# Two adaLN blocks on one core: clearing the probabilities of later keys on GpSimd, with all engines' orders written anew

## The reference

```
x = x + ga * attention0(norm(x))         # one head, no mask, softmax over 256 keys
x = x + gb * ffn0(norm(x))               # 128 -> 352 -> 128, inputs and weights rounded to blocks of fp4
x = x + ga * attention1(norm(x))         # 16 heads of 8, causal
x = x + gb * experts(norm(x))            # 4 experts of 704 in use, the best 2 weighted by a softmax
```

## Time and profile before

| | |
|---|---|
| median of 3 runs | 1906.71 us (1906.49 to 1907.74) |
| the profiled execution's own time | 1907.06 us |
| its span (first to last instruction) | 1905.3 us |
| full turns | 12, between 318.96 and 1635.28 us |
| GpSimd instructions | 78 |

### The profile page before, as it was taken

The page is one execution under the profiler, slowest core; times in us unless marked ns, Lnnn a source line. Parts: engine busy times, 40 slices in busy tenths (PEclk is TensorE's granted clock), DMA queues, the critical chain, the costliest instruction groups (busy, mean ns, idle before and its releaser), DMA issues.

```text
span 1905.3 us, 37018 instructions
## 1 busy us (share of the span) xinstructions
PE 1699.7 (89%) x12297; PEld 1317.1 (69%) x12297; DVE 1678.0 (88%) x3791; ACT 716.5 (38%) x1447; POOL 68.9 (4%) x78
## 2 busy tenths in 40 slices
PE   2347799999999999999999999999999999999998
PEld 1234567776776767677686767777676777768787
DVE  5578799989899998989989998999989899997775
ACT  0122435262533426253432526243352525334332
POOL 0000000000000000000000000000000000000000
PEclk7686899999999999999999999999999999999999
DMA  4020302003030301203030110303021030303000
GB/s 142 25 76 28 109 5 89 28 20 98 5 107 10 104 14 27 86 15 97 10 105 13 50 63 18 99 5 106 12 63 51 18 99 6 100 10 91 12 13 8
DMA packets 130106, 97.25 MB, mean 51 GB/s; under 512 B 28000, under 2 KB 124512, under 8 KB 125824
## 3 DMA queue, kind: packets, MB, share of 16 engines
q1 hardware_dynamic: 121536, 91.74, 16.4%
q10 hardware_dynamic: 8448, 4.20, 0.7%
HBM read 56.48 MB, written 29.98 MB: 45 GB/s over the span
## 4 chain that ended last, share of the span: by engine, by line
PE 47%; DVE 37%; issue 9%; ACT 4%; SPq 1%; DVEq 1%; DMA 1%; POOL 0%; ACTq 0%; POOLq 0%
DVE mneg L1099 9%; PE y_ps L1476 9%; PE bank L1469 5%; PE bank L1471 5%; PE bank L1470 5%; DVE h L1196 4%; PE bank L1220 4%; DVE tt L1188 3%; PE bank L1436 3%; ACT arena L770 2%; DVE xh L967 2%; PE bank L1343 2%; DVE arena L1107 2%; PE bank L1373 2%; PE bank L1420 2%
## 5 line engine op out<-in xcount | busy, mean ns | idle before, releaser
L813 ACT ACTIVATE tt<-bank 128x512 f32<-128x512 f32 x352 | 212.4, 603 | 665.8 <-PE bank L1471 523.9
L1476 PEld LDWEIGHTS y_ps<-wd,h 128*128 128x128 f32 (+1 forms) x3072 | 379.1, 192 | 70.7 <-issue 19.1
L1476 PE MATMUL y_ps<-wd,h 128*128 128x128 f32 (+1 forms) x3072 | 415.4, 282 | 14.1 <-DVE h L1196 14.1
L1196 DVE TENSOR_TENSOR h<-tt,bank 128x512 f32<-128x512 f32 x352 | 236.0, 682 | 23.6 <-PE bank L1471 7.1
L1188 DVE SCALAR_TENSOR_TENSOR tt<-tt,bank 128x512 f32<-128x512 f32 x352 | 237.2, 682 | 21.4 <-ACT tt L813 14.7
L1099 DVE TENSOR_REDUCE mneg<-bank 128x2 f32<-128x512 f32 (+1 forms) x384 | 236.0, 680 | 3.9 <-issue 2.4
L770 ACT ACTIVATE arena<-bank 128x512 f32<-128x512 f32 x384 | 196.5, 612 | 34.8 <-PE bank L1417 20.7
L1469 PE MATMUL bank<-h_hi,wg_hi 128*128 128x512 f32 x352 | 164.2, 466 | 10.3 <-DVE h_lo L1163 3.8
L1469 PE MATMUL bank<-h_hi,wu_hi 128*128 128x512 f32 x352 | 163.1, 463 | 8.4 <-DVE mneg L1099 8.3
L1107 DVE TENSOR_TENSOR arena<-arena,keep_k 128x1024 f32<-128x1024 f32 (+1 forms) x96 | 149.0, 1577 | 20.4 <-ACT arena L770 18.8
L1471 PE MATMUL bank<-h_lo,wg_hi 128*128 128x512 f32 x352 | 140.5, 399 | 0.0
(11 more groups left out here) (183 smaller groups left out, 2647.0 us busy)
## 6 DMA issues: line engine op xcount, KB each, us to landing
q_stack<-q_rows SPq DMA_DIRECT2D x16, 1024.0 KB, 4.8
k_stack<-k_rows SPq DMA_DIRECT2D x16, 1024.0 KB, 8.0
q_rows<-qk_halves SPq DMA_DIRECT2D x48, 256.0 KB, 2.8
k_rows<-qk_halves SPq DMA_DIRECT2D x48, 256.0 KB, 2.9
rows<-mod_rows SPq DMA_DIRECT2D x48, 128.0 KB, 3.0
rows<-mod_rows SPq DMA_DIRECT2D x16, 384.0 KB, 3.5
x_in<-in_L_attn_X SPq DMA_DIRECT2D x16, 256.0 KB, 2.8
vals<-arena SPq DMA_DIRECT2D x128, 32.0 KB, 5.2
```

Source lines behind the costliest of these rows:

```text
L813: send(a(tt[:, ch % 2, :], ps.bank(f"eg{ch}")[:], ACT.Tanh, scale=0.5), tanh_ready)
L1196: frees(v.tensor_tensor(h32[:, ch % 3], tt[:, ch % 2, :], ps.bank(f"eu{ch}")[:], ALU.mult), f"eu{ch}")
L1476: ins = mm(y_ps[:, P * t:P * (t + 1)], h32[rows_, ch % 3, P * t:P * (t + 1)], wd[rows_, ch, :], start=first and t == 0, stop=last_ and t = ...
```

## The change

`cover` moves from VectorE to GpSimd. The table `keep_k` now holds 1 where the key is allowed and 0 elsewhere. A cover is now an addition of two 4-column constants into a tile `idle` that nobody reads, a minimum with 2.0 on the blocks, a wait until that is complete, and the product with the table.

```diff
-            v.tensor_scalar(keep_k[:], code_rowf, code_col[:], HUGE, ALU.is_ge, ALU.mult)
+            v.tensor_scalar(keep_k[:], code_rowf, code_col[:], 1.0, ALU.is_ge, ALU.mult)
...
-            def cover(it, u):
-
-                dve.wait_ge(*ps.is_freed(it, f"T{TURNED[u]}{GROUPS - 1}"))
-                n = S if TURNED[u] in EARLY else P
-                x = probs[:, GROUPS * (u % 3):GROUPS * (u % 3 + 1), :].rearrange("p g (h k) -> p (g h) k", k=n)[:, :, 0:P]
-                send(v.tensor_tensor(x, x, keep_k[:].unsqueeze(1).to_broadcast([P, GROUPS * 512 // n, P]), ALU.min), covered)
...
+            def cover(it, u):
+
+                pool.wait_ge(*ps.is_freed(it, f"T{TURNED[u]}{GROUPS - 1}"))
+                n = S if TURNED[u] in EARLY else P
+                x = probs[:, GROUPS * (u % 3):GROUPS * (u % 3 + 1), :].rearrange("p g (h k) -> p (g h) k", k=n)[:, :, 0:P]
+                g.tensor_tensor(idle[:], mhalf[:], mhalf[:], ALU.add)
+                send(g.tensor_scalar(x, x, 2.0, None, ALU.min), bounded)
+                pool.wait_ge(bounded.sem, bounded.at(it, u + 1))
+                send(g.tensor_tensor(x, x, keep_k[:].unsqueeze(1).to_broadcast([P, GROUPS * 512 // n, P]), ALU.mult), covered)
```

All five orders and `USES` are written anew. The turn is cut at another place: it begins at rows 2 of lead 1, and what stood before that in the old turn stands at the end of the turn before, with a lead one higher. The orders of SyncE and GpSimd:

```diff
-    do(1, "stack_v"), do(0, "load4"), do(1, "stack_max"), do(1, "load3"), do(1, "turn_att"), do(3, "load2"), do(4, "load1")
-    do(2, "store_q"), do(2, "store_k"), do(2, "stack")
+    do(1, "load3"), do(3, "load2"), do(0, "load4"), do(1, "turn_att"), do(2, "store_q"), do(4, "load1"), do(2, "store_k")
+    do(2, "stack"), do(2, "stack_v"), do(2, "stack_max")
...
-    do(2, "stats3"), do(1, "stats4"), do(3, "stats2"), do(4, "stats1")
+    do(1, "cover", 0), do(1, "cover", 1), do(1, "cover", 2), do(1, "cover", 3), do(1, "cover", 4), do(1, "cover", 5)
+    do(2, "stats3"), do(3, "stats2"), do(1, "stats4"), do(4, "stats1")
```

The new order of VectorE, its first third and its last lines:

```diff
+    do(3, "value0"), do(0, "swish", 10), do(0, "times", 10), do(0, "swish", 11), do(3, "scores0", 0), do(0, "mix", 1)
+    do(0, "times", 11), do(3, "scores0", 1), do(0, "swish", 12), do(2, "down0"), do(0, "swish", 13), do(0, "times", 12)
+    do(0, "times", 13), do(0, "swish", 14), do(1, "turn_out", 0), do(0, "times", 14), do(2, "stats3"), do(2, "norm3")
+    do(1, "turn_out", 1), do(1, "turn_out", 2), do(1, "turn_out", 3), do(0, "swish", 15), do(3, "out0"), do(3, "stats2")
...
+    do(1, "swish", 6), do(1, "swish", 7), do(1, "times", 6), do(3, "gate0", 3), do(1, "times", 7), do(3, "up0", 2)
+    do(1, "swish", 8), do(3, "up0", 3), do(4, "norm1"), do(1, "mix", 0), do(3, "quantise_h", 0, 2), do(1, "times", 8)
+    do(3, "quantise_h", 1, 0), do(3, "quantise_h", 1, 1), do(1, "swish", 9), do(1, "times", 9), do(3, "quantise_h", 1, 2)
```

The new order of TensorE, its first and its last lines:

```diff
+    do(1, "rows", 2), do(3, "scores0", 0), do(0, "down", 8), do(0, "gate", 10), do(0, "up", 10), do(0, "gate", 11)
+    do(2, "turn_h", 0), do(2, "turn_h", 1), do(1, "rows", 3), do(1, "weigh", 0), do(2, "turn_h", 2), do(0, "down", 9)
+    do(0, "down", 10), do(1, "rows", 4), do(1, "weigh", 1), do(0, "up", 11), do(2, "turn_h", 3), do(3, "scores0", 1)
+    do(1, "rows", 5), do(2, "down0"), do(0, "gate", 12), do(0, "gate", 13), do(0, "down", 11), do(3, "probs0", 0)
+    do(1, "turn_out", 0), do(0, "up", 12), do(0, "up", 13), do(0, "gate", 14), do(0, "up", 14), do(0, "gate", 15)
+    do(1, "weigh", 2), do(3, "probs0", 1), do(1, "turn_out", 1), do(1, "weigh", 3), do(1, "turn_out", 2), do(2, "turn3")
...
+    do(3, "gate0", 3), do(1, "gate", 7), do(1, "up", 6), do(1, "up", 7), do(1, "gate", 8), do(3, "up0", 2), do(1, "down", 5)
+    do(3, "up0", 3), do(1, "up", 8), do(1, "gate", 9), do(2, "rows", 0), do(1, "down", 6), do(1, "down", 7), do(4, "turn1")
+    do(2, "rows", 1), do(4, "key0"), do(4, "query0"), do(4, "value0"), do(1, "up", 9)
```

More of the change, by code:

```diff
@@ L44 @@
 NEG = -1.0e30
-HUGE = 3.0e38
 SCALE0 = float(P) ** -0.5
@@ L68 @@
 LOOPS = PAIRS - 1 - FIRST - LAST
-USES = [(1, "SB30", "D", 6), (1, "SB31", "D", 5), (1, "SB32", "D", 2), (1, "SB33", "D", 4), (2, "G3", "D", 6),
[23 rows of a table removed]
+USES = [(1, "TE10", "A", 0), (1, "TE11", "A", 1), (1, "TE12", "A", 5), (1, "TE13", "A", 6), (3, "S0", "A", 3),
[23 rows of a table added]
 def sp_order(do):
-    do(1, "stack_v"), do(0, "load4"), do(1, "stack_max"), do(1, "load3"), do(1, "turn_att"), do(3, "load2"), do(4, "load1")
-    do(2, "store_q"), do(2, "store_k"), do(2, "stack")
+    do(1, "load3"), do(3, "load2"), do(0, "load4"), do(1, "turn_att"), do(2, "store_q"), do(4, "load1"), do(2, "store_k")
+    do(2, "stack"), do(2, "stack_v"), do(2, "stack_max")
@@ L103, in pool_order @@
 def pool_order(do):
-    do(2, "stats3"), do(1, "stats4"), do(3, "stats2"), do(4, "stats1")
+    do(1, "cover", 0), do(1, "cover", 1), do(1, "cover", 2), do(1, "cover", 3), do(1, "cover", 4), do(1, "cover", 5)
+    do(2, "stats3"), do(3, "stats2"), do(1, "stats4"), do(4, "stats1")
 def act_order(do):
-    do(0, "gate", 7), do(1, "turn_max"), do(2, "gate0", 3), do(3, "turn1"), do(0, "gate", 8), do(0, "gate", 9), do(3, "key0")
-    do(0, "gate", 10), do(1, "rows", 0), do(1, "rows", 1), do(1, "rows", 2), do(3, "query0"), do(0, "gate", 11), do(1, "weigh", 0)
@@ L112, in act_order @@
-    do(1, "rows", 3), do(1, "weigh", 1), do(1, "rows", 4), do(1, "rows", 5), do(0, "gate", 12), do(2, "turn_h", 0)
-    do(1, "weigh", 2), do(1, "weigh", 3), do(2, "turn_h", 1), do(2, "turn_h", 2), do(2, "turn_h", 3), do(1, "carry")
-    do(0, "gate", 13), do(1, "turn_att"), do(3, "scores0", 0), do(0, "gate", 14), do(3, "scores0", 1), do(3, "probs0", 0)
-    do(3, "probs0", 1), do(0, "gate", 15), do(2, "turn3"), do(0, "gate", 16), do(2, "query1"), do(0, "gate", 17), do(2, "key1")
-    do(1, "turn4"), do(0, "gate", 18), do(1, "logits"), do(2, "value1"), do(0, "gate", 19), do(0, "gate", 20), do(1, "halves4")
@@ new lines, in act_order @@
+    do(1, "rows", 2), do(0, "gate", 10), do(0, "gate", 11), do(2, "turn_h", 0), do(2, "turn_h", 1), do(1, "rows", 3)
+    do(1, "weigh", 0), do(3, "scores0", 0), do(2, "turn_h", 2), do(1, "rows", 4), do(2, "turn_h", 3), do(1, "weigh", 1)
+    do(1, "rows", 5), do(3, "scores0", 1), do(0, "gate", 12), do(1, "carry"), do(0, "gate", 13), do(3, "probs0", 0)
+    do(0, "gate", 14), do(1, "weigh", 2), do(0, "gate", 15), do(3, "probs0", 1), do(1, "weigh", 3), do(2, "turn3")
+    do(1, "turn_att"), do(2, "query1"), do(0, "gate", 16), do(2, "key1"), do(0, "gate", 17), do(2, "value1"), do(0, "gate", 18)
@@ new lines, in act_order @@
+    do(1, "turn4"), do(1, "logits"), do(0, "gate", 19), do(0, "gate", 20), do(1, "halves4"), do(0, "gate", 21), do(1, "gate", 0)
+    do(1, "gate", 1), do(3, "turn2"), do(1, "gate", 2), do(3, "gate0", 0), do(3, "gate0", 1), do(1, "gate", 3), do(1, "gate", 4)
+    do(0, "finish"), do(1, "gate", 5), do(2, "turn_max"), do(3, "gate0", 2), do(1, "gate", 6), do(1, "gate", 7), do(3, "gate0", 3)
+    do(1, "gate", 8), do(1, "gate", 9), do(2, "rows", 0), do(4, "turn1"), do(2, "rows", 1), do(4, "key0"), do(4, "query0")
@@ L347, in adaln_two_blocks @@
         mask_q, keep_k = sb("mask_q", [P, P], BF16), sb("keep_k", [P, P])
-        mhalf = sb("mhalf", [P, TILES])
+        mhalf, idle = sb("mhalf", [P, TILES]), sb("idle", [P, TILES])
         class Norm:
@@ L408, in adaln_two_blocks @@
         m_stacked = signal("m_stacked", 2 * GROUPS, 16)
-        covered = signal("covered", len(TURNED))
+        covered, bounded = signal("covered", len(TURNED)), signal("bounded", len(TURNED))
         rows_back = signal("rows_back", TILES, 16)
@@ L646, in stats4 @@
                 root(it, n3, var3_ready, rstd3_ready, 1)
-            turns(pool, pool_order, dict(stats1=stats1, stats2=stats2, stats3=stats3, stats4=stats4))
+            def cover(it, u):
[6 more added lines that the diff above has]
+                send(g.tensor_tensor(x, x, keep_k[:].unsqueeze(1).to_broadcast([P, GROUPS * 512 // n, P]), ALU.mult), covered)
+            turns(pool, pool_order, dict(cover=cover, stats1=stats1, stats2=stats2, stats3=stats3, stats4=stats4))
         @block.scalar
@@ L1208, in _ @@
                             quantise_x=quantise_x, gate0=gate0, up0=up0, quantise_h=quantise_h, down0=down0, norm3=norm3,
-                            query1=query1, key1=key1, turn_max=turn_max, maxima=maxima, cover=cover, turn_out=turn_out, add3=add3,
+                            query1=query1, key1=key1, turn_max=turn_max, maxima=maxima, turn_out=turn_out, add3=add3,
                             norm4=norm4, logits=logits, route=route, halves4=halves4, begin=begin, stats1=stats1, stats2=stats2, stats3=stats3,
```

55 lines of the change are left out of this document (18 added, 37 removed), and 46 rows, old and new, of the table USES.

## The result

The changed kernel takes 2283.36 us (median of 4, 2276.98 to 2286.09) where the kernel before, run beside it, takes 1907.22: a ratio of 1.197, 95% interval 1.195 to 1.200. The prediction said 1874 us and 1838 to 1940.

What follows compares the result with a forecast made beforehand. TensorE and VectorE were taken as nearly full, TensorE's 103.3 us flooring a 109.7 us turn. Twelve turns -38.4, partly filled turns -3, filling +6, draining +3 sum to -32.4: 1874 us, range 1838 to 1940.

Steps and rivals of the forecast that it cites:

- What bounds the kernel: Steady turns: TensorE and VectorE nearly full, 103.3 and 102.3 of 109.5 us; a turn can't fall far below 103.3.
- 3.2 us a turn: Gain per steady turn: 1.3 us from the wait for the minimum, 1.9 us from waits behind other VectorE work.
- TensorE's and ScalarE's work stays: Steady turn: only VectorE's work falls, from 102.3 to 93.0 us; the other two engines' work is unchanged.
- The new orders, costed at nothing: The rearranged written orders of the engines cost nothing, up to 1 us a turn if norm3 is late.
- has the same instructions: The turn of the loop is cut elsewhere but keeps its instructions; no cost was given to that.
- GpSimd's price: Six covers a turn on GpSimd take 25.5 us, between 17 and 44, priced from a memset pass.
- Latency: Covers reach the weighs in time in steady turns; at GpSimd's upper end they come 7.5 us late a turn.
- rival b: Slower: GpSimd's latency lies on the path of the weighs, about 1970 us; chance 0.12.
- Contention: VectorE and GpSimd blocking each other beside the covers costs 4 us a turn, between nothing and 12.
- Rival (c): Slower: VectorE blocked during the covers, 12 us a turn, 1937 us; chance 0.11.
- Filling and draining: Start and end of the run: +6 us (0 to 16) in filling, +3 us (0 to 8) in draining.
- both slower rivals: GpSimd's latency at the weighs, about 1970 us, chance 0.12; VectorE blocked during the covers, 1937 us, chance 0.11.

Runs made afterwards that it cites:

- e12: The kernel before, its own orders and bank table, with the clearing left out: 1899.15 us, ratio 0.996.
- e2: The changed kernel with the clearing left out, GpSimd doing only the short add and signalling at once: 2053.62 us, ratio 1.077.
- e9: The changed kernel without the clearing, the loop's cut moved back to the last maxima on TensorE, VectorE and ScalarE: 2012.77 us, ratio 1.056.
- e3: The changed kernel with the clearing replaced by a chain of short GpSimd adds meant to last as long as a cover: 2244.82 us, ratio 1.178.
- e20: The changed kernel without the clearing, GpSimd's two passes on a separate tile, the weighing waiting only for ScalarE's last exponential: 2275.29 us, ratio 1.193.
- e21: The kernel before, its orders, without the clearing, GpSimd's two passes on a separate tile, nothing but the roots waiting for them: 2144.50 us, ratio 1.124.

## Why the prediction was wrong, point by point

- **What bounds the kernel** was half right. TensorE's 103.3 us a turn are the bound before, but "3.2 us a turn" as the gain from VectorE's relief was wrong: e12 measures 0.6 us a turn (109.7 to 109.1). A wait put down to VectorE, in a written order of two nearly full engines, is no promise that less VectorE work removes it.
- **"TensorE's and ScalarE's work stays"** held for the instructions and not for the time. TensorE is busy 111.1 us a turn and not 103.3, at a granted clock of 0.91 for 1.00 in the twelve turns; the sum had no term for it.
- **The new orders, costed at nothing**: the first large error. They cost 148 us (e2), 41 of it the cut of the loop, which I had dismissed with "has the same instructions" (e9). The 107 us left are 5.5 us a turn (115.2 against 109.7, 66 us) and the rest in filling and draining: the first root of layer 1 comes at 226.1 us in e9 and at 213.5 before. In the turns 43 of the 66 us are TensorE's busy time at the lower clock, 23 its idle time; which steps of the orders bring it about no run here shows.
- **GpSimd's price**: 25.5 us a turn, measured 43.5. The product, at two memset passes (1.8 and 3.6), took 2.36 and 4.58. The Trainium skill (GPSIMD Engine Reference, 3.1) states 4497 ns for a two-input addition over 2048 columns, and the trace agrees. The bound, at one memset pass (0.9 and 1.8), took 2.77 and 5.35 unheld: three passes, beyond my upper end of two. The upper end of the sum, 44, held by chance.
- **Latency** (rival b): at 44 us I had 7.5 us late a turn. In the changed kernel TensorE waits 0.5 us a turn at the weighing. Yet e3 shows that without the holds this latency would cost some 191 us, at the weighing and at the roots: it is hidden only in a turn that the holds have made longer.
- **Contention** was the second large error and the larger one: 4 us a turn with a top of 12; measured 294 / 16 = 18.4 us of VectorE's time for a pair, and 222 us of the kernel's (e20 against e2). I had taken the one overlap in the trace, 0.1 us beside a root of 1 us on four columns, as its price, and looked for VectorE instructions with two SBUF operands. The runs show that instructions with one SBUF operand are held as well, down to two columns, for the rest of the GpSimd instruction; they make most of the loss (the three largest groups above 195 of the 294 us). Rival (c), VectorE blocked during the covers, was the right mechanism at 0.11 and at 12 us, with its sign in the wrong instructions. The Trainium skill (SBUF, State Buffer, the summary of rules) has the block until the first has ended, for two SBUF inputs or a two-port mode; the prediction quotes this and then counts only the first kind. For the one-input operations the trace agrees with the block's length (5.56 us for 0.53), for two-input ones beside the bound it does not: they go on 1.87 us before its end. That the held one-input operations are in the mode that the skill names, no run shows.
- **Filling and draining**, at +6 and +3 us: the second root comes at 363.3 us and not at 314.9, and behind the fourteenth stand 321.8 us and not 274.2. That is 96 us; e2 has 40 of them (337.9 and 291.0).
- **The chances**: both slower rivals stopped at or under 1970 us, since each was priced alone and the orders had no case of their own.

## What to carry to other kernels

Before moving elementwise work to GpSimd, list every elementwise VectorE instruction (with a constant, of two tensors, or a copy) with operands only in SBUF that will run beside it, whatever its size, and price each at the rest of the GpSimd instruction; a two-column scale at the head of a chain is then worth 5 us. Reduces and batch statistics were not held here. Measure first what deleting the work altogether gives (here 7 us): for the orders as they are, that is the ceiling. Price an order made anew as a change of its own, with the place where the loop is cut: here 41 us went when it was cut among the maxima. And where an order makes TensorE wait, look at its granted clock too: here its own busy time grew by 121 us.

## What the runs showed of the hardware that I had not expected

- GpSimd's one-input minimum with a constant over 128x2048 fp32 is slower than its two-input product: 5.35 us against 4.58 (2.77 and 2.36 over 1024).
- GpSimd's instruction is lengthened in turn, by a VectorE instruction that is under way when it starts: the bound over 2048 columns took 6.07 us in the 11 places where a two-input operation of 0.89 us (L862) had begun 0.03 us before it, and 5.35 in the 21 others, with a held two-column scale beside it too.
- Whether and how long a VectorE operation in SBUF is held goes by its form and by GpSimd's: to the end for nearly every operation with a constant (5.56 us for 0.53) and, beside the product, for a copy of 4 columns (L967, 14 of 14); for a two-input one to the end beside the product and until 1.87 us before the end beside the bound; not at all for a reduce or batch statistics. Open is why scales of 44 columns with one input do otherwise beside the bound: in the changed kernel 3 of 14 (L849) kept their time, in e21 13 (L857) went on 1.88 us before its end.
- Behind the loop's branch VectorE stood 2.08 and 1.55 us with its inputs ready; cut among the maxima, e9 shows 5.8 us of such waits in ten turns before its last maxima.
